# Exponent masks written into PSUM by ScalarE in the second pass of a four-part transformer block, with GpSimd's masked copies put first

## What is computed

```python
x = x + tanh(g_xattn[0]) * attention(layernorm(x), ctx, ctx)                 # 16 heads of 16, no mask
x = x + tanh(g_ffn[0])   * fp8_gemm(layernorm(x))
x = x + tanh(g_xattn[1]) * projected_attention(layernorm(x), ctx, ctx, mask) # 16 heads of 16
x = x + tanh(g_ffn[1])   * ternary_gemm(fake_quant(layernorm(x) * gamma + beta))
# in the projected attention:
scores = einsum('bhqd,bhkd->bhqk', qh, kh) / sqrt(16)
scores = where(mask[:, None] == 0, -1e9, scores)      # one 128 x 128 mask for all heads of an item
attn = softmax(scores, axis=-1)
```

## Time and profile before

| | us |
|---|---|
| time, median of 3 runs (2465.0 to 2468.1) | 2465.34 |
| profiled execution, its time | 2460.99 |
| profiled execution, its span | 2459.2 |
| TensorE busy | 2168.4 (88%) |
| VectorE busy | 1611.5 (66%) |
| ScalarE busy | 1430.5 (58%) |
| GpSimd busy | 1129.2 (46%) |

### The profile page before, as it was taken

One profiled execution on the slowest core, in us unless ns is written; L12 is line 12 of the kernel. 1 busy time (PEld: TensorE's weight loads), 2 busy tenths in 40 slices (PEclk: granted clock), 3 DMA queues, 4 the chain that ended last, 5 costly groups with the idle time before them and its releaser, 6 DMA issues. The chain is left out here.

```text
span 2459.2 us, 74014 instructions
## 1 busy us (share of the span) xinstructions
PE 2168.4 (88%) x25884; PEld 1537.5 (63%) x25884; DVE 1611.5 (66%) x3702; ACT 1430.5 (58%) x2375; POOL 1129.2 (46%) x1905
## 2 busy tenths in 40 slices
PE   3888888888888859999999999999999999999957
PEld 2666666666666547667666766666666666666635
DVE  4888888888888845555555555555554555555569
ACT  1788787887877734444444444544544444544469
POOL 2666666666666633433343343434333433434320
PEclk6999999999999979999999999999999999999989
DMA  2111111111111000000000000000000000000025
GB/s 70 45 40 43 40 41 43 40 41 42 39 43 43 15 21 21 21 18 21 18 21 18 19 20 18 21 18 21 17 21 18 21 18 18 21 18 21 4 85 189
DMA packets 95564, 80.56 MB, mean 33 GB/s; under 512 B 11392, under 2 KB 95360, under 8 KB 95360
## 3 DMA queue, kind: packets, MB, share of 16 engines
q1 hardware_dynamic: 95360, 77.44, 10.4%
HBM read 60.63 MB, written 16.78 MB: 31 GB/s over the span
## 5 line engine op out<-in xcount | busy, mean ns | idle before, releaser
L553 ACT ACTIVATE probs<-bank_exp 128x1024 f32<-128x1024 f32 x512 | 523.8, 1023 | 679.0 <-ACTq L552 679.0
L787 DVE TENSOR_REDUCE a_nmax<-bank_max 128x8 f32<-128x1024 f32 x512 | 625.7, 1222 | 330.9 <-DVEq L786 326.2
L1044 PE MATMUL bank_max<-UM,U 32*128 32x256 f32 x4096 | 588.7, 405 | 4.6 <-PEq L1079 2.5
L1051 PE MATMUL bank_exp<-UM,U 32*128 32x256 f32 x4096 | 531.1, 377 | 0.0
L510 POOL TENSOR_TENSOR ff_y<-ff_y,gamma_bc 128x256 f32<-128x256 f32 x128 | 92.8, 725 | 804.8 <-POOLq L509 804.8
L1068 PE MATMUL bank_o<-probs,V 128*17 128x128 f32 x8192 | 324.2, 275 | 127.4 <-PEq L1064 126.9
L1051 PEld LDWEIGHTS bank_exp<-UM,U 32*128 32x128 f32 x4096 | 391.9, 185 | 0.6
L1068 PEld LDWEIGHTS bank_o<-probs,V 128*17 128x17 f32 x8192 | 187.7, 96 | 275.7 <-issue 275.3
L1044 PEld LDWEIGHTS bank_max<-UM,U 32*128 32x128 f32 x4096 | 354.3, 186 | 8.6 <-issue 7.9
L1165 PE MATMUL bank_t<-spare,wT 128*128 128x128 f32 x2048 | 259.1, 280 | 0.9 <-PEq L1162 0.9
L1165 PEld LDWEIGHTS bank_t<-spare,wT 128*128 128x128 f32 x2048 | 241.3, 194 | 1.6 <-issue 1.6
(11 more groups left out here) (163 smaller groups left out, 4151.6 us busy)
## 6 DMA issues: line engine op xcount, KB each, us to landing
ctx<-in_ctx SPq DMA_DIRECT2D x256, 128.0 KB, 2.1
X<-in_x SPq DMA_DIRECT2D x128, 128.0 KB, 2.1
out_y<-X SPq DMA_DIRECT2D x64, 256.0 KB, 2.1
ff_qq<-in_mask_BxSxS_ik SPq DMA_DIRECT2D x128, 64.0 KB, 1.8
X<-in_L_xattn_Wq SPq DMA_DIRECT2D x1, 256.0 KB, 2.7
X<-in_L_xattn_Wk SPq DMA_DIRECT2D x1, 256.0 KB, 3.1
X<-in_L_xattn_Wv SPq DMA_DIRECT2D x1, 256.0 KB, 3.8
X<-in_L_xattn_Wo SPq DMA_DIRECT2D x1, 256.0 KB, 4.2
```

Of the source, the lines that this page charges most:

```text
L553: nc.scalar.activation(a_probs[n], exp_pair[:, :, :, :].rearrange("p i h t -> p (i h) t"), ACT.Exp, scale=SCALE).then_inc(probs_made, 1)
L787: return v.tensor_reduce(a_nmax[:, k2, n * H // 2:(n + 1) * H // 2], max_pair[:, :, :, :].rearrange("p i h t -> p (i h) t"), axis=AX.X, op ...
L1044: last = mm(max_pair[:, r % 2, 2 * c:2 * c + 2, :], U[now][32 * r:32 * r + 32, c, :], UM[now][32 * r:32 * r + 32, DC + c, :, :], start=not ...
L1051: last = mm(exp_pair[:, r % 2, 2 * c:2 * c + 2, :], U[before][32 * r:32 * r + 32, DC + c, :], UM[before][32 * r:32 * r + 32, c, :, :], sta ...
```

## The change

The exponent masks are no longer added by matmuls. TensorE transposes the bf16 mask once per item, next to the shift (a fifth transpose). ScalarE copies shift and mask together (640 columns instead of 512) and then, ahead of each `fill`, writes the transposed mask for all eight heads into `exp_pair` in PSUM (`seed_exp`, 128 x 1024 fp32 from a 128 x 128 bf16 tile read eight times). TensorE accumulates on it: exponent products first, the shift matmuls last, and they raise `scores`. Two matmuls before the pass write both banks of `exp_pair` once (`primed`). `probs_made` is raised by ScalarE in an instruction of its own, after it has waited for its own exponential, and TensorE waits for `exp_seeded` ahead of both fills. The maximum masks stay matmuls.

GpSimd makes the masked copies ahead of the bias addition and of gamma and beta, and raises `qk_read` when U is there; the input transposes wait for that, and `fill(0, ...)` of the next step waits for `m_made`. On VectorE the aggregates and the `absmax` reduction move behind the addition that makes `U`, ahead of the second maximum.

```diff
@@ -113,7 +113,9 @@
         V = [sb(f"V{n}", [P, H, VW], FP32) for n in range(RING)]
         sh = sb("sh", [P, 4 * P], BF16)[:, :]
         ones_b = sb("ones_b", [P, P], BF16)[:, :]
-        sh_T = [sb(f"sh_T{n}", [P, 4 * P], BF16)[:, :] for n in range(2)]
+        sh_mask_T = [sb(f"sh_T{n}", [P, 5 * P], BF16)[:, :] for n in range(2)]
+        sh_T = [t[:, 0:4 * P] for t in sh_mask_T]
+        mask_T = [t[:, 4 * P:5 * P] for t in sh_mask_T]
@@ -501,6 +508,15 @@
                     if live(3):
                         nc.gpsimd.tensor_tensor(a_shift[:, s, 2:4], a_shift[:, s, 2:4], a_rstd[:, s, 2:4], ALU.mult)\
                           .then_inc(n1_made, 1)
+                if live(1):
+                    s = (k + 1) % RING
+                    pool.wait_ge(u_made, 1)
+                    pool.sem_inc(u_made, -1)
+                    pool.sem_inc(qk_read, 1)
+                    mine(nc.gpsimd.tensor_scalar(UM[s][:, :, 0, :], U[s][:, :, :], heads_eo[:, 0:1], 0.0,
+                                                 ALU.mult, ALU.add))
+                    nc.gpsimd.tensor_scalar(UM[s][:, :, 1, :], U[s][:, :, :], heads_eo[:, 1:2], 0.0,
+                                            ALU.mult, ALU.add).then_inc(m_made, 1)
                 if live(0):
                     mine(nc.gpsimd.tensor_tensor(xs(i), xs(i), bo_bc[:, :], ALU.add))
                 if live(-7):
@@ -510,16 +526,6 @@
                     mine(nc.gpsimd.tensor_tensor(n2[k % 2], n2[k % 2], gamma_bc[:, :], ALU.mult))
                     settle()
                     nc.gpsimd.tensor_tensor(n2[k % 2], n2[k % 2], beta_bc[:, :], ALU.add).then_inc(n2_scaled, 1)
-                if live(1):
-                    s = (k + 1) % RING
-                    pool.wait_ge(u_made, 1)
-                    pool.sem_inc(u_made, -1)
-                    if live(0):
-                        settle()
-                    mine(nc.gpsimd.tensor_scalar(UM[s][:, :, 0, :], U[s][:, :, :], heads_eo[:, 0:1], 0.0,
-                                                 ALU.mult, ALU.add))
-                    nc.gpsimd.tensor_scalar(UM[s][:, :, 1, :], U[s][:, :, :], heads_eo[:, 1:2], 0.0,
-                                            ALU.mult, ALU.add).then_inc(m_made, 1)
@@ -602,14 +608,38 @@
             act.drain().then_inc(pass_ends[0], 1)
             act.wait_ge(pass_ends[0], 5)
 
+            act.wait_ge(primed, 1)
+            act.sem_inc(primed, -1)
+
+            def seed_exp(ring):
+
+                nc.scalar.activation(exp_pair[:, :, :, :].rearrange("p i h t -> p (i h) t"),
+                                     mask_T[ring].rearrange("p (o t) -> p o t", o=1).broadcast_to([P, H // 2, P]),
+                                     ACT.Copy).then_inc(exp_seeded, 1)
+
+            def exp_settled(n):
+                act.wait_ge(scores, 1)
+                act.sem_inc(scores, -1)
+                nc.scalar.activation(a_probs[n], exp_pair[:, :, :, :].rearrange("p i h t -> p (i h) t"), ACT.Exp,
+                                     scale=SCALE).then_inc(act_own, 1)
+
+            def probs_settled():
+
+                act.wait_ge(act_own, 1)
+                act.sem_inc(act_own, -1)
+                act.sem_inc(probs_made, 1)
+
             def step_b(i, k, live):
                 odd = k % 2 == 1
                 if live(-2):
-                    exp_pair_of(1)
+                    exp_settled(1)
                 if live(-1):
                     act.wait_ge(shift_Td, 1)
                     act.sem_inc(shift_Td, -1)
-                    nc.scalar.activation(sh_T[(k + 1) % 2], bank_tb[1][:, 0:4 * P], ACT.Copy).then_inc(shift_out, 1)
+                    nc.scalar.activation(sh_mask_T[(k + 1) % 2], bank_tb[1][:, 0:5 * P], ACT.Copy).then_inc(shift_out, 1)
+                if live(-2):
+                    probs_settled()
+                    seed_exp(k % 2)
                 if not odd and live(2):
                     act.wait_ge(n1_made, 1)
                     act.sem_inc(n1_made, -1)
@@ -631,12 +661,21 @@
                                          bank_m[:, 0:D].rearrange("p (h d) -> p h d", d=DH), ACT.Copy)\
                       .then_inc(v_out, 1)
                 if live(-2):
-                    exp_pair_of(0)
+                    exp_settled(0)
                 if live(-3):
                     act.wait_ge(cn_T, 1)
                     act.sem_inc(cn_T, -1)
                     nc.scalar.activation(cn_nT.rearrange("p c t -> p (c t)"), bank_t[1][:, D:2 * D], ACT.Copy)\
                       .then_inc(cn_out, 1)
+                if live(-1):
+                    if live(-2):
+                        probs_settled()
+                    else:
+                        act.wait_ge(mask_T_made, 1)
+                        act.sem_inc(mask_T_made, -1)
+                    seed_exp((k + 1) % 2)
+                elif live(-2):
+                    probs_settled()
@@ -892,6 +931,28 @@
                     vec.sem_inc(y_read, 1)
                 if live(5):
                     n_bn = mine(v.bn_stats(st6_b[n][:, 0:6], xs(i + 5)))
+                if live(0):
+                    max_pair_of(0, k % 2).then_inc(max_read, 1)
+                if live(-3):
+                    vec.wait_ge(attn_back, 1)
+                    vec.sem_inc(attn_back, -1)
+                    mine(v.reciprocal(rden[:, :], bank_oh[:, :, DH]))
+                    settle()
+                    attn_normed().then_inc(attn_read, 1)
...
+                    v.tensor_tensor(U[(k + 1) % RING][:, :, :], bank_t[0][:, :].rearrange("p (c t) -> p c t", c=4),
+                                    bqk_T[:, :].rearrange("p (c o) -> p c o", o=1).broadcast_to([P, 4, P]),
+                                    ALU.add).then_inc(u_made, 1)
                 if odd and (live(5) or live(-5)) and (live(1) or live(-9)):
                     vec.wait_ge(pair_read, 1)
                     vec.sem_inc(pair_read, -1)
@@ -915,32 +976,10 @@
                     vec.sem_inc(n2_scaled, -1)
                     last = v.tensor_reduce(col(absmax, i - 8), n2[(k + 1) % 2], axis=AX.X, op=ALU.max,
                                            apply_absolute_value=True)
-                    if live(-7 + 1):
+                    if live(-6):
                         last.then_inc(n2_used, 1)
                     else:
                         mine(last)
-                if live(0):
-                    max_pair_of(0, k % 2).then_inc(max_read, 1)
-                if live(-3):
...
-                                    ALU.add).then_inc(u_made, 1)
                 if live(0):
                     n_max = mine(max_pair_of(1, k % 2))
                     settle(n_max)
@@ -1026,24 +1065,27 @@
                     last = nc.tensor.transpose(bank_o[:, g * P:(g + 1) * P], attn_T[:, g, :], identf[:, :])
                 last.then_inc(attn_back, 1)
 
-            def fill(n, now, before, ring, mask_now=None, mask_before=None):
-
-                masked = mask_now is not None or mask_before is not None
+            def fill(n, now, before, ring, seeded=False, mask=None):
+
                 lo, hi = 2 * n, 2 * (1 - n)
-                if now is not None and masked:
+                if now is not None and seeded:
                     for b in range(2):
-                        mm(max_pair[:, b, :, :], ident[:, :], mask_now.rearrange("p (o t) -> p o t", o=1)
+                        mm(max_pair[:, b, :, :], ident[:, :], mask.rearrange("p (o t) -> p o t", o=1)
                            .broadcast_to([P, HG, P]), start=True, stop=False, skip_group_check=True)
-                if before is not None:
+
+                def add_shift(start):
                     for r in (hi, hi + 1):
-                        mm(exp_pair[:, r % 2, :, :], ones_b[32 * r:32 * r + 32, :],
-                           sh_T[ring][32 * r:32 * r + 32, :], start=True, stop=False, skip_group_check=True)
+                        last = mm(exp_pair[:, r % 2, :, :], ones_b[32 * r:32 * r + 32, :],
+                                  sh_T[ring][32 * r:32 * r + 32, :], start=start, stop=False, skip_group_check=True)
+                    return last
+                if before is not None and not seeded:
+                    add_shift(True)
                 for c in range(DC):
                     if now is not None:
                         for r in (lo, lo + 1):
                             last = mm(max_pair[:, r % 2, 2 * c:2 * c + 2, :], U[now][32 * r:32 * r + 32, c, :],
                                       UM[now][32 * r:32 * r + 32, DC + c, :, :],
-                                      start=not masked, stop=True, skip_group_check=True)
+                                      start=not seeded, stop=True, skip_group_check=True)
                         if c == DC - 1:
                             last.then_inc(max_scores, 1)
                     if before is not None:
@@ -1051,13 +1093,11 @@
                             last = mm(exp_pair[:, r % 2, 2 * c:2 * c + 2, :], U[before][32 * r:32 * r + 32, DC + c, :],
```

(40 more changed lines are left out.)

33 lines of the change are left out of this document (16 added, 17 removed).

## The result

The change made the kernel faster, by less than forecast: 2400.44 us median of 4 runs (2398.4 to 2402.6) against 2465.17 for the kernel before on the same chip (4 runs, 2465.0 to 2468.1). The ratio is 0.9735, with a 95% interval of 0.9718 to 0.9752. The forecast was 2373, its range 2335 to 2405: 65 us were gained where 92 were expected. The profiled execution took 2399.2 us with a span of 2397.2, 62.0 less than the span of 2459.2 before.

A forecast was written before the change was run, and what follows sets the result against it. TensorE was taken to bound the second pass. A gain of 0.575 us per item x 128 = 74, plus 19 for m_made, minus 1 once, made 92 us: 2369 profiled, 2373 as median, range 2335 to 2405.

The forecast's parts named there:

- Four mask matmuls leave, the transposes' load is exposed, one transpose comes: Per item on TensorE: exponent-mask matmuls save 0.97 us, an exposed attention-transpose load costs 0.06, the bf16 mask transpose 0.055.
- Shift at the end, 0.20 a step: In both TensorE fills, moving the shift matmuls last exposes a load at the exponent products' start: 0.10 us each.
- Second release 0.08: Raising probs_made separately after ScalarE's wait on itself delays weighing of pair 0 by 0.08 us per item.
- `m_made`, 19 us: Input transposes no longer wait for GpSimd's masked copies on every second step: 0.30 us on 64 steps, 19 us gained.
- Slacks of the seeds, 0.1 and 0.3: Spare time before TensorE would wait for ScalarE's seeds: 0.1 us after fill(1), 0.3 after fill(0).
- x 128: Second pass: the net gain of 0.575 us per item multiplied by all 128 items, giving 74 us.
- 2350 to 2388 by its own terms: Whole kernel: the range in us for the forecast as summed, given a chance of 0.58.
- the edges: Weight loads exposed where exponent products start in the two fills: 0.20 us per item, bounds 0 and 0.40.
- rival 2: Seeds of 1.25 us, or queued waits, make TensorE's fills late: 2390, or 2414 with seeds of 1.38; chance 0.14.
- Rivals 1, 3 and 4: rival 1, rival 3, and a fourth: half-rate seeds make TensorE wait for exp_seeded, slower than before, 2542, chance 0.05.
- rival 1: The load in the fills hides and probs_made's second release is free: 36 us more saved, 2337; chance 0.17.
- rival 3: Input transposes wait for xn, put back by a ScalarE seed, instead of for GpSimd: 2392; chance 0.04.

The follow-up runs named there:

- the first experiment: The changed kernel with the two shift matmuls back at the head of each fill: 2378.0 us, ratio 0.9617.
- the order alone: The kernel before with only the new order of GpSimd and VectorE and its moved waits, exponent masks still by matmuls: 2448.7 us, ratio 0.9919.
- seeds alone: The changed kernel with the old order on GpSimd and VectorE, m_made awaited ahead of the input transposes: 2508.7 us, ratio 1.016.

## Why the prediction was right, and where it was off

- *Four mask matmuls leave, the transposes' load is exposed, one transpose comes:* right. The stream after shows 0.056 for the mask's transpose (1601.85 to 1601.91) and no matmul behind the shift.
- *Shift at the end, 0.20 a step:* right, 0.108 in each fill, and undone by the first experiment for 0.20. The shift's own load hides: it starts 0.21 behind the product in the same rows. The rule of the Trainium skill that was set aside ("TensorE: Matmul & The Clock Gate", section "The mechanism") would have had it exposed; the trace disagrees with it once more.
- *Second release 0.08:* 0.12 (1.49 between the weighings instead of 1.37).
- *`m_made`, 19 us:* right, though each late step gave 0.35 and not 0.30; alone the new order gained 19 us (2468.1 to 2448.7), and no wait takes its place. The cover was there as forecast: the copies end at 1606.51, the next fill starts at 1609.44.
- *Slacks of the seeds, 0.1 and 0.3:* the first was 0.27. For the second only the trace after speaks: the seed ends at 1603.87 (1602.84 + 1.03), the fill starts at 1604.61, 0.74 later, and with the same 0.29 for the release 0.45 is left. No steady step waits for either seed.
- *The step that failed:* "x 128". It took all items for steady steps, and 19 of the 127 between the first and the last copy were not. The 13 turns, which should have gained 7.5 (13 x 0.575, for none of them is a late step), lost 9.2, and the last steps lost 7.4. Both places could be seen in the trace before, as idle time at 13 turns (2.27 us in the one shown above) and as the 0.55 us of idle time at 2320.29, where the projections under which the seed's slack was counted had stopped. That is the term that was mis-sized: 92 us stood there, and 62 to 65 were measured.
- *The bounds:* the sum's "2350 to 2388 by its own terms" is narrower than the bounds that it is said to come from: the edges alone, 0 to 0.40 a step, make 2347 to 2399. And the range does not take in all of rival 2, whose second price is 2414. The result lies outside 2350 to 2388, and inside 2335 to 2405 only by the room kept for rival 2, which is not what happened; that much is luck.
- *Rivals:* 2390 and 2414 of rival 2 lie on either side of the result, but its mechanism (seeds of 1.25 us, waits for `exp_seeded` in most steps) is not what happened: seeds take 1.03, and in the second pass TensorE waits at the turns and in the first and last steps, not in the steady ones. Rivals 1, 3 and 4 did not occur. The bound of nothing for the edges (rival 1) was reached only by putting the shift first. A sentence under rival 3 proved to matter more than its price: the seed ahead of `xn` and `n2` puts GpSimd back by a microsecond, which is harmless with the new order; with the old one the kernel takes 108 us more (2508.7 against 2400.4).

Left open: why the clock falls behind every turn after the change and behind fewer than half before. It falls behind 6 of 6 turns in the kernel before with 16 steps, at 2.40 us of idle time, and not behind several of 2.5 to 2.7 us before; the length of the stop alone does not decide. What the branch waits for in its 3.3 to 4.1 us was not measured either.

## What to carry to other kernels

Split a gain per item into the steps that are really alike, those at a turn of a hardware loop, and those at either end of a pipeline, and read each kind's idle time and clock in the trace before multiplying. A chain that hides under one part of the work (here the seed for `fill(1, ...)` under the projection matmuls) is bare in the steps where that part is missing, so use the old way there. Where a queue gets new work in front of something, price what is queued behind it on the other engines too: two edits may pay only together.

## What the runs showed of the hardware

- A turn of the loop costs TensorE 3.3 to 4.1 us of branch, whether the body holds 8, 16 or 56 steps (3.6 on average with 8; with 16, 3.5 in the kernel before and 3.7 in the changed one; 3.7 at the one turn with 56). I had not expected it to be the largest loss left in the pass.
- Waits one behind another on TensorE's queue cost 0.15 us each right behind the branch of a turn: from the end of the branch to the first matmul it is 0.17 us with one wait (the kernel before), 0.32 at most turns with two (the order alone) and, again at most turns, 0.47 with three. In steady steps they cost nothing (10.131 us with three ahead of the fill, 10.129 with two of them moved behind the mask matmuls).
- A small operation of VectorE can be held up by GpSimd. L989 writes 128 x 16 elements; it took 230 ns before and takes 716 after (715 with the order alone), now that it starts beside GpSimd's addition of beta, and both end together. Timelines of VectorE and of GpSimd:

```profile
1608.04 0.75 DVE L989 TENSOR_TENSOR sh<-a_nmax,sh 128x16 bf16<-128x16 f32 x1
```

```profile
1607.97 0.73 POOL L528 TENSOR_TENSOR ff_y<-ff_y,beta_bc 128x256 f32<-128x256 f32 x1
```

With the old order (seeds alone) it takes 240 ns again, and the cast ahead of it, which then stands beside a masked copy, takes 508 instead of 209. It lies off the path that sets the step here. The Trainium skill ("SBUF — State Buffer", section "SBUF: two separate sides") says that GpSimd and a VectorE operation with two inputs in SBUF take a shared pair of ports for the whole of an instruction, and the other waits; the trace agrees, with ends at 1608.79 and 1608.70.
